# Low half of the experts' second weight brought by DMA, and the image products split over the two halves of the output partitions

## The chip, the cores and the metric

The kernel runs on one core of one Trainium2 chip. The metric is device time in microseconds of one execution, from several runs of the same program. A profile is one further execution, recorded by the hardware profiler. The engines are TensorE (PE in the profile, its weight loads PEld), VectorE (DVE), ScalarE (ACT), GpSimd (POOL) and SyncE (SP), which here only issues transfers.

## The reference, cut to what matters

Thirty-two samples of 153 tokens (25 image patches, 128 text tokens) with 192 channels are embedded, go through a quantised attention block and then through a mixture of three experts, of which one is taken for each sample:

```python
scores = softmax(mean(x, axis=1) @ Wg.T)              # x: [32, 153, 192]
sel = top_k(scores, 1)                                # one of 3 experts per sample
h = gelu(einsum('bth,ehf->betf', x, W1) + b1)         # F = 768
y = einsum('betf,efh->beth', h, W2) + b2
out = einsum('beth,be->bth', y, scores * one_hot(sel, 3))
h = h_residual + out
```

The kernel computes the expert that was taken, and no other. Float32 products are made of bf16 parts: a value is split into a high part and the remainder (the low part), and the products high x high, high x low and low x high are accumulated in PSUM.

## The kernel before, in words

The program goes through nine stages, with all engines meeting at the end of each: embedding, scales of the inputs, ranges of the hidden values, quantised q, k and v, ranges of the scores, attention, projection, the inputs of the experts (`ffn_inputs`), and `experts`. The change touches `experts` alone, which fills the last 170 us.

In `experts` every engine walks over the 32 samples (called rows here, n = 0 to 31) in an order written out by hand: `steps` writes four rows out, then a hardware loop of four rows a turn, then the last step. In step n an engine does its first job for row n and its second job for row n-1. Semaphores alone tie the engines together.

- **SyncE** (`weights`, L1824 to L1830): reads the number of the row's expert from the tile `sel` into a register (L1826, a TENSOR_LOAD in the trace), waits until row n-4's first product is done, and copies the row's first weight, high and low half, from its resident place (`vt` in the trace) into slot n mod 4 of a ring (`qk`), with two transfers of 128 x 2 x 768 bf16 (L1830). They add 16 each to the slot's semaphore `w_in`. Then `rows` (L1832) waits for row n-4's output and sends it out (L1834), and after every fourth row the image tile of the last four rows (L1838).
- **TensorE** (`first_product`, L1857): 30 matmuls of 153 columns make the 768 hidden values of the row in six chunks (L1867). `second_product` (L1871), for the row before: 18 matmuls of 192 columns (L1878) make the 128 text tokens' output in PSUM tile `p2`, from the split hidden values `gs` (`e_gs` in the trace) and the resident second weight, whose high half is `w2h` (`vbd` in the trace) and whose low half is `w2l` (`kb`). The expert is picked in both by a register in the address. Then 12 matmuls of 192 columns (L1883) make the image part: the stationary operand `gs[:, u, f, BOTH]` has 64 columns, 32 with the high part of the image tokens and 32 with their low part, and so the output lies on partitions 0 to 63 of `p3`, high part's products on 0 to 31 and low part's on 32 to 63. The last one raises `y_acc`. Before them PE waits for `i_bias`, before the 18 for `g_split` (the split hidden values) and `y_bias`.
- **ScalarE** (L1906): six GELU activations per row. Every second row starts with a table load.
- **VectorE**: `split(n)` (L1929) makes `gs` in three instructions, a cast (L1935) and two subtractions (L1937, L1938). `collect(n-1)` (L1942) reads the expert's number into a register (L1944, a TENSOR_LOAD), then adds the bias to the text output in `p2` (L1947), the bias to the image output in `p3[0:32]` (L1950), scales the text output and adds the residual (L1953), and adds `p3[32:64]` to the image tile `yi` (L1955). `yi` has 32 partitions for each of four rows, at 32*j with j = n mod 4. After j = 3, `image` (L1957) finishes the tile for four rows (L1960).

In the trace the tiles `yb`, `ot`, `yi` and `oi` all appear as `vi`, the ring of the first weight and ScalarE's output as `qk`, and all three PSUM tiles as `e_p`.

Of the kernel before, what the change touches and what calls it, by code (L numbers as in the profile page):

```python
# [7 lines left out]
ALU = mybir.AluOpType  # L8
ACT = mybir.ActivationFunctionType
F32 = mybir.dt.float32  # L10
BF16 = mybir.dt.bfloat16
# [7 lines left out]
P = 128  # L19
B, NI, NT = 32, 25, 128  # L20
# [4 lines left out]
C = 192  # L25
# [8 lines left out]
FT = FF // P  # L34
# [25 lines left out]
class Ctx:  # L60
# [8 lines left out]
    def sb(self, name, shape, dt=F32, stack=None):  # L69
        return (stack or self.stack).enter_context(self.nc.sbuf_tensor(name, shape, dt))  # L70
# [298 lines left out]
def wait_apart(eng, sem, value, passed):  # L369

    eng.wait_ge(sem, value)
    eng.sem_inc(passed, 1)
# [1410 lines left out]
def experts(k, m):  # L1783

    out, Hres = k.d["out"], m["H"]
    X, w1h, w1l, w2h, w2l, sel, gw, gwi, b2, b1s = (m[x] for x in ("X", "w1h", "w1l", "w2h", "w2l", "sel", "gw", "gwi", "b2", "b1s"))
    RING = SLOTS = 4

    HI, BOTH, LO = slice(0, NT), slice(IW, IW + 64), slice(N + 32, N + 32 + NT)
    with ExitStack() as st:  # L1790
        sb = lambda n, s, t=F32: k.sb(n, s, t, st)
        g = m["qkflat"][:, 12288:12288 + 4 * FT * N].bitcast(F32).rearrange("p (u f n) -> p u f n", u=2, f=FT)
        gs = sb("e_gs", [P, 2, FT, N + 32 + NT], BF16)
        ws = m["qkflat"][:, 0:SLOTS * 4 * FF].rearrange("p (s i a f) -> p s i a f", s=SLOTS, i=2, a=2)
        rows_out = m["vi"][:, :, :].rearrange("p a b -> p (a b)").bitcast(F32).rearrange("p (t c) -> p t c", c=C)
        share = m["line"][:, :, :].rearrange("p a b -> p (a b)")[:, 0:2 * FT * B].rearrange("p (e f b) -> p e f b", e=2, f=FT)
# [24 lines left out]
        with k.nc.Block() as block:  # L1821
            @block.sync
            def _(sp):
                def weights(n, u):  # L1824

                    e = sp.value_load(sel[0:1, ds(n, 1)], min_val=0, max_val=E - 1)  # L1826
                    if not (isinstance(n, int) and n < SLOTS):
                        wait_apart(sp, h_acc, (n - SLOTS) * 2 + 2, k.passed)
                    for i, w in enumerate((w1h, w1l)):
                        sp.dma_start(ws[:, u, i, :, :], w[:, :, e, :]).then_inc(w_in[u], 16)  # L1830

                def rows(n, j, grp):  # L1832
                    wait_apart(sp, y_out, n + 2, k.passed)
                    sp.dma_start(out[n, NI:N, :], ot[:, j, :]).then_inc(sent[j], 16)  # L1834
                    if j == 3:
                        wait_apart(sp, i_out, grp + 2, k.passed)
                        for q in range(4):
                            sp.dma_start(out[grp * 4 + q, 0:NI, :], oi[32 * q + ID:32 * q + 32, :]).then_inc(image_sent, 16)  # L1838

                def body(c, kk):  # L1840
                    now, gone = batch(c, kk, 0), batch(c, kk, 4)
                    if now is not None:
                        weights(now[0], now[1])
                    if gone is not None:
                        rows(*gone)
                steps(sp, body)
                for n in range(B - 3, B):
                    rows(n, n % 4, n // 4)
                for q in range(4):
                    sp.wait_ge(sent[q], 16 * G + 16)  # L1850
                sp.wait_ge(image_sent, 64 * G + 64)

            @block.tensor
            def _(pe):
                expert = lambda n: pe.value_load(sel[0:1, ds(n, 1)], min_val=0, max_val=E - 1)

                def first_product(n, kk):  # L1857

                    u = kk % 2
                    pe.wait_ge(h_act, n * FT + FT)  # L1860
                    pe.wait_ge(w_in[kk], (n - kk) * 8 + 32)
                    for f in range(FT):
                        o = p1[:, u, f // 3, (f % 3) * N:(f % 3 + 1) * N]
                        fs = slice(f * P, (f + 1) * P)
                        parts = ((0, 0, 0), (1, 0, 0), (0, 0, 1), (0, 1, 2), (1, 1, 2))
                        for a, (w, kt, plane) in enumerate(parts):
                            mm = pe.matmul(o, ws[:, kk, w, kt, fs], X[:, plane, ds(n * N, N)], start=(a == 0), stop=(a == len(parts) - 1))  # L1867
                        if f % 3 == 2:
                            mm.then_inc(h_acc, 1)

                def second_product(n, slot, e):  # L1871
                    pe.wait_ge(g_split, n * 2 + 2)

                    pe.wait_ge(y_bias, n + 1)
                    u = slot % 2
                    parts = [(a, w, f) for f in range(FT) for a, w in ((HI, w2h), (HI, w2l), (LO, w2h))]
                    for b, (a, w, f) in enumerate(parts):
                        mm = pe.matmul(p2[:, u, 0:C], gs[:, u, f, a], w[:, e, f, :], start=(b == 0), stop=(b == 3 * FT - 1))  # L1878

                    wait_apart(pe, i_bias, n + 1, k.passed)  # L1880
                    parts = [(w, f) for f in range(FT) for w in (w2h, w2l)]
                    for b, (w, f) in enumerate(parts):
                        mm = pe.matmul(p3[0:64, u, 0:C], gs[:, u, f, BOTH], w[:, e, f, :], start=(b == 0), stop=(b == 2 * FT - 1))  # L1883
                    mm.then_inc(y_acc, 1)

                def body(c, kk):
                    now, last = batch(c, kk, 0), batch(c, kk, 1)
                    e_last = expert(last[0]) if last is not None else None
                    if now is not None:
                        first_product(now[0], now[1])  # L1890
                    if last is not None:
                        second_product(last[0], last[1], e_last)
                steps(pe, body)
# [16 lines left out]
            def _(v):  # L1910
# [31 lines left out]
                def collect(n, j, grp):  # L1942
                    u, r = j % 2, slice(32 * j, 32 * j + 32)
                    e = v.value_load(sel[0:1, ds(n, 1)], min_val=0, max_val=E - 1)  # L1944
                    v.wait_ge(y_acc, n + 1)
                    v.wait_ge(y_out, n + 1)
                    v.tensor_tensor(yb[:, u, :], p2[:, u, 0:C], b2[:, e, :], ALU.add).then_inc(y_bias, 1)  # L1947

                    v.wait_ge(i_out, grp + 1)
                    v.tensor_tensor(yi[r, :], p3[0:32, u, 0:C], b2[0:32, e, :], ALU.add).then_inc(i_half, 1)  # L1950
                    v.wait_ge(y_bias, n + 3)
                    v.wait_ge(sent[j], (n - j) * 4 + 16)
                    v.scalar_tensor_tensor(ot[:, j, :], yb[:, u, :], gw[:, ds(n, 1)], Hres[:, n, :], ALU.mult, ALU.add).then_inc(y_out, 1)  # L1953
                    v.wait_ge(i_half, n + 1)
                    v.tensor_tensor(yi[r, :], p3[32:64, u, 0:C], yi[r, :], ALU.add).then_inc(i_bias, 1)  # L1955

                def image(grp):  # L1957
                    v.wait_ge(i_bias, grp * 4 + 6)
# [140 lines left out]
```

## Time and profile before

| | |
|---|---|
| median of 3 runs | 1036.82 us |
| lowest and highest | 1031.38 us, 1037.0 us |
| the profiled execution's own time | 1037.42 us |
| its span, first to last instruction | 1035.6 us |
| mean granted clock of TensorE | 0.837 |
| busy in the span | PE 707.6, DVE 881.2, ACT 711.9, POOL 170.0 us |
| `experts` in the span | from about 865 us to the end |

The profiled execution's time is 1.8 us more than its span, which begins and ends with an instruction, and 0.6 us above the median. Busy time is time in which an engine executes instructions of its own; reading a register, waiting and issuing transfers are not in it, and in the timeline and the chain of waits they appear with a q behind the engine's name or as "issue". Granted clock 1.0 is 2.4 GHz and 0.5 is 1.2 GHz.

### The profile page before, as it was taken

What the parts mean: (1) busy time and instruction counts of PE and PEld (TensorE: products, weight loads), DVE (VectorE), ACT (ScalarE), POOL (GpSimd) and SP (SyncE); (2) the same over time, 40 slices, a digit from 0 to 9 for tenths busy, and PEclk for the clock granted to TensorE, in tenths of its full rate; (3) what the DMA queues carried; (4) which work ended last, traced back from release to release, by engine and by line L of the source; (5) the groups of instructions that cost most, each with busy time, mean ns of one, the idle gap of its engine ahead of it and who ended that gap; (6) DMA issues with size and microseconds to landing.
All of it is one profiled execution on the core that took longest, in us unless ns stands there. A gap on an engine that the chain in (4) does not pass through costs nothing. (4 is left out here: it accounts for less than half of the span.)

```text
span 1035.6 us, 22661 instructions
## 1 busy us (share of the span) xinstructions
PE 707.6 (68%) x5955; PEld 482.3 (47%) x5956; DVE 881.2 (85%) x2422; ACT 711.9 (69%) x1376; POOL 170.0 (16%) x274
## 2 busy tenths in 40 slices
PE   3783386747888366676667666676635385999997
PEld 3562244425555233443334333343323244989996
DVE  6888997888888799999999999999978864666766
ACT  0335465957888699898988889999945294555553
POOL 5851410016664000000000000000004530000000
PEclk9985598988999687778887887877756597999999
DMA  8000000001111111111111111111022004355452
GB/s 256 3 2 0 0 1 1 0 1 39 37 37 37 36 28 24 27 25 23 25 24 24 24 24 24 24 23 24 12 89 78 18 1 152 135 186 204 165 197 83
DMA packets 84271, 54.71 MB, mean 53 GB/s; under 512 B 53704, under 2 KB 83176, under 8 KB 83976
## 3 DMA queue, kind: packets, MB, share of 16 engines
q1 hardware_dynamic: 83208, 54.11, 17.2%
q0 software_dynamic: 1024, 0.13, 0.3%
q8 instruction: 18, 0.29, 0.1%
q14 instruction: 21, 0.17, 0.1%
HBM read 11.90 MB, written 3.76 MB: 15 GB/s over the span
## 5 line engine op out<-in xcount | busy, mean ns | idle before, releaser
L1357 DVE SCALAR_TENSOR_TENSOR expo<-expo,con,pow 128x153 f32<-128x153 f32 x480 | 146.1, 374 | 0.8 <-ACT expo L1266 0.8
L1140 PE MATMUL at_rem<-word,ident_half 128*128 128x459 f16 x160 | 66.4, 415 | 102.7 <-ACT expo L1266 101.5
L1266 ACT ACTIVATE expo<-at_rem,con 128x459 f32<-128x459 f32 x160 | 95.4, 640 | 14.5 <-PE at_rem L1141 13.7
L952 DVE TENSOR_REDUCE rs_ends<-rs_banks 128x770 f32 (+1 forms) x96 | 89.2, 957 | 13.5 <-PE rs_banks L924 11.4
L873 ACT ACTIVATE rs_banks<-rs_banks 128x770 f32<-128x770 f32 x96 | 74.6, 796 | 23.2 <-PE rs_banks L916 22.1
L1222 ACT ACTIVATE word<-at_banks 128x459 uint8<-128x459 f32 x160 | 81.0, 560 | 10.4 <-PE at_banks L779 10.2
L1400 DVE CUSTOM_DVE_ANT_0 weight_top<-weight_top,line 128x2448 uint16<-128x2448 uint16 x64 | 86.1, 1345 | 2.1 <-ACT line L1258 2.1
L1140 PEld LDWEIGHTS at_rem<-word,ident_half 128*128 128x128 f16 x160 | 15.7, 98 | 152.8 <-ACT expo L1266 148.1
L1258 ACT ACTIVATE line<-weight_top 128x1224 f32<-128x1224 f32 x64 | 74.0, 1158 | 15.0 <-DVE weight_top L1385 14.7
L774 PE MATMUL at_banks<-pick,row_top 128*128 128x459 bf16 x160 | 73.1, 457 | 11.0 <-ACT word L1222 4.0
L1906 ACT ACTIVATE qk<-e_p,b1s 128x153 f32<-128x153 f32 x192 | 58.9, 392 | 29.3 <-PE e_p L1867 28.1
L1867 PE MATMUL e_p<-X,qk 128*128 (+1 forms) x960 | 72.6, 235 | 7.7 <-DMA qk<-vt 6.9
L1867 PEld LDWEIGHTS e_p<-X,qk 128*128 128x128 bf16 x960 | 66.0, 100 | 13.7 <-issue 10.4
L1215 ACT ACTIVATE pT_all<-at_pT 128x768 bf16<-128x768 int16 (+2 forms) x128 | 71.8, 637 | 0.8 <-PE at_pT L1157 0.6
L1453 POOL PARTITION_ALL_REDUCE pj_mm<-pj_mm x1 | 0.4, 356 | 418.6 <-DVE pj_mm L1527 418.6
L1385 DVE TENSOR_TENSOR weight_top<-expo,inv_total 128x1224 f32<-128x1224 f32 x64 | 68.2, 1106 | 0.0
L1141 PE MATMUL at_rem<-octave,octave_step 128*128 128x459 f16 x160 | 67.8, 424 | 0.0
L1157 PE MATMUL at_pT<-identb,weight_top 128*128 128x128 bf16 x480 | 52.0, 271 | 20.8 <-ACT pT_all L1215 19.7
L1906 ACT ACT_TABLE_LOAD x16 | 20.5, 1283 | 55.4 <-PE e_p L1867 55.4
L779 PE MATMUL at_banks<-kb,qk 128*128 128x153 bf16 x384 | 56.1, 263 | 0.0
L1878 PE MATMUL e_p<-vbd,e_gs 128*128 x384 | 53.1, 246 | 3.8 <-DVE e_gs L1938 3.8
L684 ACT ACTIVATE qi<-pq,biasp,ap 128x306 int16<-128x306 f32 x96 | 48.0, 727 | 11.1 <-PE pq L642 11.1
(390 smaller groups left out, 2085.2 us busy)
## 6 DMA issues: line engine op xcount, KB each, us to landing
qk<-vt SPq DMA_DIRECT2D x64, 384.0 KB, 3.1
rs_kb<-qk SPq DMA_DIRECT2D x128, 28.7 KB, 1.9
kb<-qk SPq DMA_DIRECT2D x128, 28.7 KB, 1.9
patches<-in_patches SPq DMA_DIRECT2D x4, 768.0 KB
vi<-vt SPq DMA_DIRECT2D x32, 96.0 KB, 2.0
out<-vi SPq DMA_DIRECT2D x32, 96.0 KB, 1.8
pj_w<-in_w SPq DMA_DIRECT2D x1, 2304.0 KB, 8.2
qb<-qk SPq DMA_DIRECT2D x128, 6.0 KB, 1.8
```

The lines of the kernel that those rows point to most:

```text
L774: pe.matmul(bank[:, 0:3 * N], top, pick[:, 3 * i:3 * i + 3, :].rearrange("p w n -> p (w n)"), start=True, stop=False, skip_group_check=True)
L873: act.activation(banks[:, s, :, 0:5 * W], banks[:, s, 1, 0:5 * W].unsqueeze(1).to_broadcast([P, 2, 5 * W]), ACT.Relu).then_inc(split, 1)
L952: v.tensor_reduce(ends[:, :, n, 5 * b:5 * b + 5], banks[:, slot(u, b), :, 0:5 * W].rearrange("p i (t n) -> p i t n", n=W), AX, ALU.max).th ...
L1140: pe.matmul(out, identh[:, :], bank(word, b).bitcast(F16), start=True, stop=False)
L1215: rank = lambda out, x: act.activation(out, x.bitcast(I16), ACT.Copy, bias=RANKS)
L1222: act.activation(dist[:, 3 * b:3 * b + 3, :], banks[:, b % 3, 0:3 * N].rearrange("p (t n) -> p t n", n=N), ACT.Copy, scale=per_step).then_ ...
L1258: act.activation(flat(line, halves[h]), flat(top, halves[h]), ACT.Copy, scale=LOWER / 3.0, bias=1.5 * LOWER).then_inc(y_done, 1)
L1266: act.activation(bank(ex, b), rem[:, (u + b) % 2, 0:3 * N], ACT.Square, scale=2.0 ** 24, bias=c(5)).then_inc(sq_done, 1)
L1357: ins = v.scalar_tensor_tensor(ex[:, t, :], ex[:, t, :], c(7), pw[:, t, :].bitcast(BF16), ALU.add, ALU.mult, accum_out=tot[:, t:t + 1])
L1400: v.tensor_tensor(flat(top, half).bitcast(I32), flat(top, half).bitcast(I32), flat(line, half).bitcast(I32), ALU.add).then_inc(i_done, 1)
L1867: mm = pe.matmul(o, ws[:, kk, w, kt, fs], X[:, plane, ds(n * N, N)], start=(a == 0), stop=(a == len(parts) - 1))
L1906: act.activation(g[:, u, f, :], p1[:, u, f // 3, (f % 3) * N:(f % 3 + 1) * N], ACT.Gelu, bias=b1s[:, f, ds(n, 1)]).then_inc(h_act, 1)
```

## The change

The image part of the second product is written as six pairs. In a pair, one matmul multiplies the 64 stationary columns with the high half of the weight and writes partitions 0 to 63 of `p3`, and the other multiplies the same 64 columns with the low half and writes partitions 64 to 127. Before, both were accumulated on partitions 0 to 63. The number of matmuls, 12, and their columns stay.

The low half of the weight for this part no longer comes from `kb` through a register in the address. It is copied per row by a third transfer (128 x 1152 bf16, contiguous on each side) to one of four places `wl`: two in a new tile `e_w2_low`, two in the tile `line`. SyncE waits for `y_acc` of row n-4 before it, and `w_in` now counts 48 per turn of the ring.

On VectorE, `collect` gets one more addition per row, of `p3[64:96]` into `yi`. It waits for the addition before it. Partitions 96 to 127 of `p3`, the product of the two low parts, are not read; before, that product was part of what L1955 added.

```diff
--- before.py
+++ after.py
@@ -1791,6 +1791,9 @@
         sb = lambda n, s, t=F32: k.sb(n, s, t, st)
         g = m["qkflat"][:, 12288:12288 + 4 * FT * N].bitcast(F32).rearrange("p (u f n) -> p u f n", u=2, f=FT)
         gs = sb("e_gs", [P, 2, FT, N + 32 + NT], BF16)
+        wl_own = sb("e_w2_low", [P, 2, FT, C], BF16)
+        wl_line = m["line"][:, :, :].rearrange("p a b -> p (a b)")[:, 2 * FT * B:2 * FT * B + FT * C].bitcast(BF16).rearrange("p (u f c) -> p u f c", u=2, f=FT)
+        wl = [wl_own[:, 0, :, :], wl_own[:, 1, :, :], wl_line[:, 0, :, :], wl_line[:, 1, :, :]]
         ws = m["qkflat"][:, 0:SLOTS * 4 * FF].rearrange("p (s i a f) -> p s i a f", s=SLOTS, i=2, a=2)
         rows_out = m["vi"][:, :, :].rearrange("p a b -> p (a b)").bitcast(F32).rearrange("p (t c) -> p t c", c=C)
         share = m["line"][:, :, :].rearrange("p a b -> p (a b)")[:, 0:2 * FT * B].rearrange("p (e f b) -> p e f b", e=2, f=FT)
@@ -1828,6 +1831,9 @@
                         wait_apart(sp, h_acc, (n - SLOTS) * 2 + 2, k.passed)
                     for i, w in enumerate((w1h, w1l)):
                         sp.dma_start(ws[:, u, i, :, :], w[:, :, e, :]).then_inc(w_in[u], 16)
+                    if not (isinstance(n, int) and n < SLOTS):
+                        wait_apart(sp, y_acc, n - SLOTS + 1, k.passed)
+                    sp.dma_start(wl[u], w2l[:, e, :, :]).then_inc(w_in[u], 16)
 
                 def rows(n, j, grp):
                     wait_apart(sp, y_out, n + 2, k.passed)
@@ -1858,7 +1864,7 @@
 
                     u = kk % 2
                     pe.wait_ge(h_act, n * FT + FT)
-                    pe.wait_ge(w_in[kk], (n - kk) * 8 + 32)
+                    pe.wait_ge(w_in[kk], (n - kk) * 12 + 48)
                     for f in range(FT):
                         o = p1[:, u, f // 3, (f % 3) * N:(f % 3 + 1) * N]
                         fs = slice(f * P, (f + 1) * P)
@@ -1878,9 +1884,9 @@
                         mm = pe.matmul(p2[:, u, 0:C], gs[:, u, f, a], w[:, e, f, :], start=(b == 0), stop=(b == 3 * FT - 1))
 
                     wait_apart(pe, i_bias, n + 1, k.passed)
-                    parts = [(w, f) for f in range(FT) for w in (w2h, w2l)]
-                    for b, (w, f) in enumerate(parts):
-                        mm = pe.matmul(p3[0:64, u, 0:C], gs[:, u, f, BOTH], w[:, e, f, :], start=(b == 0), stop=(b == 2 * FT - 1))
+                    for f in range(FT):
+                        pe.matmul(p3[0:64, u, 0:C], gs[:, u, f, BOTH], w2h[:, e, f, :], start=(f == 0), stop=(f == FT - 1))
+                        mm = pe.matmul(p3[64:128, u, 0:C], gs[:, u, f, BOTH], wl[slot][:, f, :], start=(f == 0), stop=(f == FT - 1))
                     mm.then_inc(y_acc, 1)
 
                 def body(c, kk):
@@ -1951,8 +1957,10 @@
                     v.wait_ge(y_bias, n + 3)
                     v.wait_ge(sent[j], (n - j) * 4 + 16)
                     v.scalar_tensor_tensor(ot[:, j, :], yb[:, u, :], gw[:, ds(n, 1)], Hres[:, n, :], ALU.mult, ALU.add).then_inc(y_out, 1)
-                    v.wait_ge(i_half, n + 1)
-                    v.tensor_tensor(yi[r, :], p3[32:64, u, 0:C], yi[r, :], ALU.add).then_inc(i_bias, 1)
+                    v.wait_ge(i_half, n * 2 + 1)
+                    v.tensor_tensor(yi[r, :], p3[32:64, u, 0:C], yi[r, :], ALU.add).then_inc(i_half, 1)
+                    v.wait_ge(i_half, n * 2 + 2)
+                    v.tensor_tensor(yi[r, :], p3[64:96, u, 0:C], yi[r, :], ALU.add).then_inc(i_bias, 1)
 
                 def image(grp):
                     v.wait_ge(i_bias, grp * 4 + 6)
```

Where the instructions stand, before and now, at three places (rows are an engine's instructions in program order; a line number, the operation, output<-inputs and sizes; ISA and REGISTER_ALU are register work).

TensorE, from the last text matmul into the image part, in the written-out rows; before:

```order
L1878 MATMUL e_p<-vbd,e_gs 128x192
L1883 MATMUL e_p<-vbd,e_gs 64x192 [waits e_i_bias]
L1883 MATMUL e_p<-kb,e_gs 64x192
L1883 MATMUL e_p<-vbd,e_gs 64x192
L1883 MATMUL e_p<-kb,e_gs 64x192
```

and now (five further pairs follow the first):

```order
L1884 MATMUL e_p<-vbd,e_gs 128x192
L1888 MATMUL e_p<-vbd,e_gs 64x192 [waits e_i_bias]
L1889 MATMUL e_p<-e_w_low,e_gs 64x192
L1888 MATMUL e_p<-vbd,e_gs 64x192
L1889 MATMUL e_p<-e_w_low,e_gs 64x192
```

The order of high and low stays; the second of each pair reads the copied weight and writes the other half of the partitions.

VectorE, one `collect` and the start of the next `split`; before:

```order
L1944 TENSOR_LOAD sel [waits e_g_split]
L1944 ISA x2
L1947 ISA [waits e_y_out,e_y_acc]
L1947 TENSOR_TENSOR vi<-e_p,b 128x192
L1950 TENSOR_TENSOR vi<-e_p,b 32x192 [waits e_i_out]
L1953 SCALAR_TENSOR_TENSOR vi<-vi,gw,Hres 128x192 [waits e_sent0,e_y_bias]
L1955 TENSOR_TENSOR vi<-e_p,vi 32x192 [waits e_i_half]
L1935 CAST e_gs<-qk 128x6x153 [waits e_y_acc,e_h_act]
```

and now:

```order
L1950 TENSOR_LOAD sel [waits e_g_split]
L1950 ISA x2
L1953 ISA [waits e_y_out,e_y_acc]
L1953 TENSOR_TENSOR vi<-e_p,b 128x192
L1956 TENSOR_TENSOR vi<-e_p,b 32x192 [waits e_i_out]
L1959 SCALAR_TENSOR_TENSOR vi<-vi,gw,Hres 128x192 [waits e_sent0,e_y_bias]
L1961 TENSOR_TENSOR vi<-e_p,vi 32x192 [waits e_i_half]
L1963 TENSOR_TENSOR vi<-e_p,vi 32x192 [waits e_i_half]
L1941 CAST e_gs<-qk 128x6x153 [waits e_y_acc,e_h_act]
```

One instruction, L1963, stands between the old last addition and the next row's cast.

SyncE, one turn of the loop's first row; before:

```order
L1830 ISA [waits e_h_acc]
L1830 DMA qk<-vt 128x2x768
L1830 ISA
L1830 DMA qk<-vt 128x2x768
L371 REGISTER_ALU
L1834 ISA [waits e_y_out]
L1834 DMA out<-vi 128x192
```

and now:

```order
L1833 ISA [waits e_h_acc]
L1833 DMA qk<-vt 128x2x768
L1833 ISA
L1833 DMA qk<-vt 128x2x768
L371 REGISTER_ALU
L1836 ISA [waits e_y_acc]
L1836 DMA e_w_low<-kb 128x1152
L371 REGISTER_ALU
L1840 ISA [waits e_y_out]
L1840 DMA out<-vi 128x192
```

The third transfer and its wait stand between the first weight's transfers and the sending of a finished row.

## Rows read from the trace of the kernel before

**Rows 1.** The page: busy time, and the chain that ended last by engine.
```profile
PE 707.6 (68%) x5955; PEld 482.3 (47%) x5956; DVE 881.2 (85%) x2422; ACT 711.9 (69%) x1376; POOL 170.0 (16%) x274
...
PE 10%; issue 2%; DVE 2%; ACT 1%; DVEq 1%; DMA 0%; SPq 0%; ACTq 0%
```

**Rows 2.** Busy time by windows: stretch, length, each engine's busy us, clock, DMA share, GB/s.
```profile
893.00:1031.00 138.00, 133.69 (x1665) 121.89 (x1662) 95.75 (x207) 67.40 (x179) 0.00 (x0) 1.00 0.48 169
243.00:342.00 99.00, 78.93 (x736) 54.17 (x734) 88.43 (x99) 87.15 (x129) 54.29 (x140) 1.00 0.18 36
```

**Rows 3.** Timeline of PE, one row: start us, us, engine, line, operation.
```profile
926.35 0.25 PE L1878 MATMUL e_p<-vbd,e_gs 128*128 x1
...
927.93 0.27 PE L1883 MATMUL e_p<-vbd,e_gs 128*64 x1
...
928.86 0.25 PE L1883 MATMUL e_p<-kb,e_gs 128*64 x1
929.04 2.17 PE L1867 MATMUL e_p<-X,qk 128*128 x30
931.05 0.25 PE L1878 MATMUL e_p<-vbd,e_gs 128*128 x1
```

**Rows 4.** Timeline of DVE, j = 0 and j = 1; idle before in brackets.
```profile
922.51 0.36 DVE L1947 TENSOR_TENSOR vi<-e_p,b 128x192 f32<-128x192 f32 x1 [1.06 <-issue]
...
923.57 0.35 DVE L1955 TENSOR_TENSOR vi<-e_p,vi 32x192 f32<-32x192 f32 x1
923.85 0.62 DVE L1935 CAST e_gs<-qk 128x918 bf16<-128x918 f32 x1
...
927.13 0.36 DVE L1947 TENSOR_TENSOR vi<-e_p,b 128x192 f32<-128x192 f32 x1 [1.40 <-issue]
...
927.90 0.42 DVE L1953 SCALAR_TENSOR_TENSOR vi<-vi,gw,Hres 128x192 f32<-128x192 f32 x1
928.35 0.35 DVE L1955 TENSOR_TENSOR vi<-e_p,vi 32x192 f32<-32x192 f32 x1
928.73 0.64 DVE L1935 CAST e_gs<-qk 128x918 bf16<-128x918 f32 x1
```

**Rows 5.** Timeline of DVE: casts of four rows, an early one, the last bias.
```profile
884.55 0.64 DVE L1935 CAST e_gs<-qk 128x918 bf16<-128x918 f32 x1 [2.49 <-ACT qk L1906]
...
919.56 0.64 DVE L1935 CAST e_gs<-qk 128x918 bf16<-128x918 f32 x1
...
933.59 0.64 DVE L1935 CAST e_gs<-qk 128x918 bf16<-128x918 f32 x1 [0.34 <-ACT qk L1906]
...
938.74 0.63 DVE L1935 CAST e_gs<-qk 128x918 bf16<-128x918 f32 x1
...
1030.52 0.36 DVE L1947 TENSOR_TENSOR vi<-e_p,b 128x192 f32<-128x192 f32 x1 [0.46 <-PE e_p L1883]
```

**Rows 6.** Waits of DVE, 893 to 1032 us: who <- whom, us in total, times, longest.
```profile
DVE vi L1947 <- issue: 32.8, 28, 1.5
DVE e_gs L1935 <- ACT qk L1906: 3.1, 7, 0.7
```

**Rows 7.** The line that reads the expert's number on DVE: ns min/median/max.
```profile
L1944 DVEq TENSOR_LOAD <-sel x32: 300/311/778, 879.6 to 1029.4; - x32
```

**Rows 8.** Start of the stage in the chain; a smaller transfer from the page.
```profile
865.82 0.75 SPq L1830
...
866.71 3.11 DMA qk<-vt
...
vi<-vt SPq DMA_DIRECT2D x32, 96.0 KB, 2.0
```

**Rows 9.** Timeline of PE in the attention, 64 stationary columns.
```profile
499.86 0.32 PE L1173 MATMUL at_out<-pT_all,v_image_row 128*64 128x128 bf16 x2
499.97 0.23 PE L1174 MATMUL at_out<-pT_all,v_image_row 128*64 128x25 bf16 x2
```

**Rows 10.** Windows, columns as in rows 2: the clock there.
```profile
499.40:502.60 3.20, 3.07 (x28) 1.83 (x27) 3.20 (x18) 2.66 (x6) 0.00 (x0) 0.50 0.07 24
```

## Prediction

> **What bounds the kernel now.** The page comes first: VectorE is busy for most of the span, yet the chain that ended last runs over TensorE, and shares of a whole program say little about its last stage [rows 1]. So the windows view is read for this stage: in 138 us TensorE is busy 133.7, VectorE 95.8 and ScalarE 67.4, with the clock at its upper level throughout [rows 2]. By busy time alone TensorE is the limit and VectorE has 42 us to spare. The timelines of the two engines say otherwise.
>
> TensorE's row [rows 3]: from the first text matmul at 926.35 to the first image matmul at 927.93 is 1.58 us, from there to the next row's first product at 929.04 is 1.11, and from there to the next text matmul at 931.05 is 2.01. A row takes 4.70 us, four rows 18.8. The twelve image matmuls start 0.085 us apart ((928.86 - 927.93)/11 = 0.93/11), and 0.18 us pass from the last of them to the first product.
>
> VectorE's row: cast to cast is 923.85 - 919.56 = 4.29 us in the step that collects a row with j = 0, then 928.73 - 923.85 = 4.88, then 4.86 with a wait of 0.34 for ScalarE in it, then 5.15, which has the image instruction [rows 4, 5]. Four rows take 938.74 - 919.56 = 19.18 us, and of these VectorE waited for another engine for 0.34. What looks like idle time is not slack: the 1.06 or 1.40 us before each L1947 [rows 4] is called "issue", it sums to 32.8 us over 28 rows [rows 6], and it is the sequence that reads the expert's number, with a register load of 0.30 to 0.78 us in it [rows 7]. It stands in every row, also in those in which nothing was late. So VectorE's own sequence needs 19.18 - 0.34 = 18.84 us for four rows, and TensorE's 18.8: **two engines are at the limit together**. Over the whole stretch VectorE waited for ScalarE 3.1 us in 7 places [rows 6]; that is all it has left.
>
> **TensorE's part of the change.** Twelve matmuls become six pairs on separate halves of the output partitions. The attention has such pairs: two matmuls with 64 stationary columns form one piece of 0.32 us, and the next two begin 0.11 us later (499.86 to 499.97) [rows 9]. The clock was at its lower level, 1.2 GHz [rows 10], where 128 columns need 0.107 us, so the pair took the time of one matmul. I take the same here: six pairs at 0.085 us, 5 intervals instead of 11, and the image part goes from 1.11 to about 0.60 us. It saves 0.51 us a row; TensorE's row becomes 4.20 us, four rows 16.8. The bounds are 0 (the pairs run one behind the other) and 0.51.
>
> **VectorE's part.** One addition of 32 x 192 is added per row. Its nearest row is L1955, 0.35 us, with the same shapes and the same tiles [rows 4]. What it adds to the row is the distance from one start to the next. The rows show two cases: at 923.57 the next instruction starts after 0.28 us, at 928.35 after 0.38 [rows 4], so the bounds are 0.28 and 0.38. I take 0.38, because the new instruction waits for the one ahead of it, and its input is on other partitions than that one's, as where L1955 follows L1953 (0.42 long, start to start 0.45).
>
> The Trainium skill has a rule for just this ("VectorE: DVE Perf Modes", section "Two Vector instructions with no wait between them"): an instruction starts only after all earlier ones have finished if its input or output starts in another group of 32 partitions than the last one's from the same memory, and may otherwise start earlier. The rows agree: short distances only where the tile's quarter is the first, long ones elsewhere. By the rule the new addition is held in every row (its input starts at partition 64, the last one's at 32), and 32 rows cost 12.2 us; if it weren't held, 9.0.
>
> Now the cover. 32 additions by 0.38 are 12.2 us on VectorE. Off it come the waits that they fill: 3.1 us for ScalarE [rows 6]; the first row's addition, which lies in the wait of 2.49 us before 884.55 [rows 5], 0.4; the start of the third first product, which follows the first, shortened image part, 0.5, and brings that wait's end forward; and the wait for TensorE before the last L1947, 0.46 [rows 5], of which 0.4 is filled while TensorE comes earlier. That is 4.4, and **7.8 us are left**. TensorE's 0.51 us a row buys nothing else: with 16.8 us against VectorE's 18.84 + 4 x 0.38 = 20.4 for four rows, it will wait about 0.9 us in each row for the split values.
>
> **SyncE and the transfers.** The third transfer is 288 KB, between 96 KB, which lands in 2.0 us, and 384 KB, which lands in 3.1 [rows 8]. In the first row it delays the start, since TensorE waits for three transfers: the chain goes over the second one's landing, and one issue takes 0.75 us and 0.89 from start to start (865.82 to 866.71) [rows 8]. So the start comes about **0.8 us later**; bounds 0 and 1.5 (issue and data behind each other). Later rows hide it. It waits for row n-4's second product, two rows, some 10 us, before row n's first product; behind it SyncE has only the sending of row n-4, which waits for VectorE's later work on the same row anyway. One more issue of 0.75 us beside two fits into a row of 5 us. Cover gone, a late weight would cost its lateness once per row.
>
> The transfer has a second effect. The idle before L1947 is 1.06 in one row and 1.40 in the next [rows 4]; (32.8 - 28 x 1.06)/0.34 gives some 9 long ones of 28. The long ones come while weights are in flight. The DMA share rises from 0.48 [rows 2] by 288/768 of nearly all of it, to about 0.6. I count no change in the number of long loads, since the third transfer is issued at another place of the row; the bounds are 9 fewer (-3 us) and 20 more (+7 us).
>
> **The sum** is 7.8 + 0.8 = 8.6 us against the profiled execution's 1037.42, so 1046.0. That execution is 0.6 us above the median, and for the median I forecast 1036.8 + 8.6 = **1045.4 us**. What a measurement of this kernel can tell from no change is about 1%, 10.4 us: the forecast lies inside, not far from its edge (1047.2).
>
> **Rivals.** (1) *VectorE has slack after all*, chance 0.07. The idle stretches would shrink under pressure, and TensorE's gain would appear: some 28 rows by 0.51 less 0.8, so 1023 us. For it speaks the chain, which names mostly TensorE [rows 1]; against it that 1.06 us recurs where all inputs were there, and the 19.18 against 18.84 above. It decides if VectorE can do four rows with the additions in under 18.8 us.
>
> (2) *The register load becomes long in most rows*, chance 0.17. The third transfer would be in flight when VectorE reads the number; 20 more long loads at 0.34 are 6.8 us, so 1052. It passes the edge of 1% from about 5 more long loads on. Against it: the median load is short today, 311 ns [rows 7], though transfers take half the time. The Trainium skill ("DMA: Bandwidth & Descriptors", section "Latency and other measured facts") gives such a load a floor of about 600 ns; by that all would be long already, and the trace, with 300 ns, disagrees.
>
> (3) *The pairs don't overlap*, the change doing nothing for TensorE, chance 0.05. TensorE's 18.8 us for four rows is still under VectorE's 20.4; only the two gains at the start and the end go, +0.9, so 1046.3.
>
> (4) *A weight arrives late or TensorE's clock falls*, chance 0.06 in all. TensorE idle for 0.9 us of 5.1 would be busy 0.82 of the time. In the ranges stage it was busy 0.80 of 99 us with the clock at its upper level [rows 2]. One fall over a row would cost that row some 4 us; a weight late by 1 us in each row would end at 1070.
>
> The forecast itself has 0.63, between 1041 and 1049; 0.02 is left for a gain that I don't see. From these: faster by over 1% 0.08 (rival 1 and part of the rest), within 1% 0.55 (four fifths of the forecast, most of rival 3), slower by over 1% 0.37. The range for 8 in 10 leaves out rival 1 and the worst of 4 and takes in rival 2 and the low bounds (9 short loads, a start that isn't later): 1038 to 1053 us.
>
> **What the profile after would show.** Right: L1963 in 32 instances of about 0.35 us with about 0.03 us before it; cast to cast of four rows 20.0 to 20.8 us; no wait of VectorE for ScalarE past the first rows; the image part of TensorE 0.6 us long, and before each first text matmul a wait of nearly 1 us for VectorE's L1944; the chain mostly on VectorE and issue; the first product starting 0.8 us later. Wrong: idle before VectorE's bias addition under 1 us (rival 1) or 1.4 in most rows (rival 2), image matmuls 0.085 us apart (rival 3), first products waiting for a transfer after the first row (rival 4).

## The result, and the profile after the change

| | before | after |
|---|---|---|
| median of the runs | 1036.70 us (4 runs) | 1049.61 us (4 runs, 1048.05 to 1050.5) |
| ratio, 95% interval | | 1.0122 [1.0106, 1.0138] |
| span of the profiled execution | 1035.6 us | 1046.2 us |
| first register load of SyncE to the end | 170.75 us | 184.79 us |

The change costs **12.9 us** in the medians, 1.2%, inside the range and with the sign of the forecast, 4.3 us more than the 8.6 of its sum: the additions on VectorE are the cost, as forecast, and the cover that was taken off them did not come. This is just over the bound of 1%. The stage itself is 14.0 us longer. The profiled execution began it 3.4 us earlier (861.46 against 864.87 us), which has nothing to do with the change; so parts of the stage are compared below, not whole spans.

The page after, busy time and chain; they answer to [rows 1]:

```profile
PE 695.0 (66%) x5955; PEld 464.6 (44%) x5956; DVE 892.1 (85%) x2454; ACT 710.9 (68%) x1376; POOL 167.2 (16%) x274
...
issue 6%; DVE 6%; DVEq 3%; PE 1%; DMA 0%; ACT 0%; SPq 0%; ACTq 0%
```

TensorE, 10% of the chain before, has 1%. VectorE, its queue and "issue" have the rest. The windows view after, columns as in [rows 2]: the middle of the stage and its last product.

```profile
893.00:1041.00 148.00, 125.03 (x1649) 107.01 (x1647) 104.39 (x232) 66.30 (x175) 0.00 (x0) 0.99 0.57 206
```
```profile
1036.70:1040.00 3.30, 3.22 (x22) 2.80 (x24) 1.83 (x5) 0.00 (x0) 0.00 (x0) 0.50 0.06 19
```

The DMA share rose from 0.48 to 0.57. In the last product the granted clock was 0.50, the lower level, after TensorE had waited up to 2.6 us for VectorE. The waits after, 893 to 1041 us, which answer to [rows 6]:

```profile
DVE vi L1953 <- issue: 34.6, 28, 1.6
...
PE e_p L1873 <- issue: 11.2, 24, 0.7
PE e_p L1884 <- DVE e_gs L1944: 9.9, 20, 2.6
```

VectorE's waits for ScalarE have gone from this stretch. TensorE waits 9.9 us for VectorE's split values, and 11.2 us for nothing but its own queue, in front of the first product. The second of these waits was not foreseen. VectorE's timeline over two rows (start, duration, line), which answers to [rows 4, 5]:

```profile
940.83 0.63 DVE L1941 CAST e_gs<-qk 128x918 bf16<-128x918 f32 x1
...
951.01 0.64 DVE L1941 CAST e_gs<-qk 128x918 bf16<-128x918 f32 x1
951.68 0.96 DVE L1943 TENSOR_TENSOR e_gs<-qk,e_gs 128x768 bf16<-128x768 f32 x1
952.56 0.35 DVE L1944 TENSOR_TENSOR e_gs<-qk,e_gs 128x192 bf16<-128x192 f32 x1
954.12 0.36 DVE L1953 TENSOR_TENSOR vi<-e_p,b 128x192 f32<-128x192 f32 x1 [1.21 <-issue]
954.51 0.35 DVE L1956 TENSOR_TENSOR vi<-e_p,b 32x192 f32<-32x192 f32 x1
954.90 0.42 DVE L1959 SCALAR_TENSOR_TENSOR vi<-vi,gw,Hres 128x192 f32<-128x192 f32 x1
955.34 0.35 DVE L1961 TENSOR_TENSOR vi<-e_p,vi 32x192 f32<-32x192 f32 x1
955.73 0.35 DVE L1963 TENSOR_TENSOR vi<-e_p,vi 32x192 f32<-32x192 f32 x1
956.33 0.64 DVE L1941 CAST e_gs<-qk 128x918 bf16<-128x918 f32 x1 [0.24 <-issue]
...
961.87 0.63 DVE L1941 CAST e_gs<-qk 128x918 bf16<-128x918 f32 x1
```

Four rows take 961.87 - 940.83 = 21.04 us (before 19.18, forecast 20.4, and 20.0 to 20.8 among the signs of being right). The new addition L1963 starts 0.39 us after L1961, as forecast. One thing is new: the cast at 956.33 comes 0.60 us after L1963 instead of 0.38, with 0.24 of "issue", and the loop's branch stands there. The 1.56 us between the starts of L1944 and L1953 are not new in kind: the same stretch took 1.29 to 1.88 us before, and its sum over 31 rows rose from 46.9 to 50.0 us. TensorE's timeline at an image part, which answers to [rows 3]:

```profile
944.48 0.27 PE L1888 MATMUL e_p<-vbd,e_gs 128*64 x1
944.48 0.27 PE L1889 MATMUL e_p<-e_w_low,e_gs 128*64 128x192 bf16 x1
944.59 0.25 PE L1888 MATMUL e_p<-vbd,e_gs 128*64 x1
944.59 0.25 PE L1889 MATMUL e_p<-e_w_low,e_gs 128*64 128x192 bf16 x1
...
944.92 0.25 PE L1889 MATMUL e_p<-e_w_low,e_gs 128*64 128x192 bf16 x1
945.47 1.23 PE L1873 MATMUL e_p<-X,qk 128*128 x15 [0.31 <-issue]
```

The two halves start at the same time, pairs are 0.08 to 0.11 us apart, six pairs start within 0.44 us. And yet 0.99 us pass from the image part's start to the next first product, at best from the third row on (0.62 us stands once, in the second row); the median from 893 us on is 1.20 us, where it was 1.11. The start of the stage in the chain, and VectorE's register load, which answer to [rows 8] and [rows 7]:

```profile
863.27 0.64 SPq L1833
864.04 3.08 DMA e_w_low<-kb
867.12 0.14 issue
867.26 2.10 PE e_p L1873 x15
```
```profile
L1950 DVEq TENSOR_LOAD <-sel x32: 301/358/1048, 877.3 to 1039.5; - x32
```

From SyncE's first register load to the first product it is 867.26 - 861.46 = 5.80 us, before 5.08. The register load's mean rose from 422 to 486 ns, the worst from 778 to 1048.

### The profile page after: what moved, and what is told of

It reads as the page before. It is cut to its first block and busy times, and to the rows that moved or that the text cites. A ratio compares the mean times of both kernels' runs of the same rounds, so it can differ in the third digit from the quotient of the medians.

```text
span 1046.2 us, 22827 instructions
## 1 busy us (share of the span) xinstructions
PE 695.0 (66%) x5955; PEld 464.6 (44%) x5956; DVE 892.1 (85%) x2454; ACT 710.9 (68%) x1376; POOL 167.2 (16%) x274
## 5 line engine op out<-in xcount | busy, mean ns | idle before, releaser
L1873 PE MATMUL e_p<-X,qk 128*128 (+1 forms) x960 | 73.6, 236 | 22.0 <-issue 12.9
L1157 PE MATMUL at_pT<-identb,weight_top 128*128 128x128 bf16 x480 | 52.2, 271 | 20.8 <-ACT pT_all L1215 19.8
L1884 PE MATMUL e_p<-vbd,e_gs 128*128 x384 | 55.3, 250 | 11.0 <-DVE e_gs L1944 10.9
```

## The experiments

Twelve kernels, in three groups. Each group shared its runs of the kernel before (1036.76, 1037.36 and 1036.20 us). "Theory V", "theory A" and so on are names that each expectation explains. Two numbers are read from each trace beside the time: the **24 rows** from the sixth to the thirtieth cast, as the mean of four rows (before 19.53 us, after 21.07), and the distance from the start of an image part to the next first product (median from 893 us on, before 1.11, after 1.20).

**The change taken apart: additions and transfer.** First the two halves put into the kernel before, each alone.

```
a3, before with a second addition        a4, before with the third transfer
+ tensor_tensor(yi, p3[32:64], yi)       + dma_start(wl[u], w2l[:, e]) in SyncE's weights()
                                           (wl is brought and not read)
```

> The kernel before with one more addition per row on VectorE: p3[32:64] is added to the image tile a second time, each waiting for the one ahead (so the image part of the output counts that piece twice). Theory V (VectorE's own sequence sets the row): four rows take 18.5 us with short register loads plus 4 x 0.385, so 20.1 to 20.7 us, and the run is 8 to 10 us slower than before, nearly all of what the change costs; TensorE's image part stays at 1.11 us. Theory T (the third transfer is the cost, by long register loads and a late start): this run has no such transfer and is within 3 us of before.

Measured: 1049.55 us, ratio 1.0122 [1.0108, 1.0136], four rows 20.94 us. The additions alone give 12.8 us (1049.55 - 1036.76), as much as the whole change, and more than the 8 to 10 us of theory V; the four rows, too, lie above its 20.1 to 20.7.

> The kernel before with the third transfer per row and its wait for y_acc, and w_in counted with it; nobody reads what it brings. Theory V: the start is 0.7 us later and the register loads on VectorE cost up to 0.1 us a row more, so 1 to 4 us slower. Theory T: 8 to 13 us slower.

Measured: 1040.37 us, 1.003 [1.0008, 1.0052], four rows 20.13 us: 3.6 us, within theory V's 1 to 4, though not for its reasons, as shown below. Then the change without the one or the other (a1 leaves out the product rows of partitions 64 to 95, a2 takes the low half of expert 0 in every row):

```
a1  - tensor_tensor(yi[r, :], p3[64:96, u, 0:C], yi[r, :], ALU.add)
a2  - dma_start(wl[u], w2l[:, e, :, :])
    - matmul(p3[64:128, u], gs, wl[slot][:, f, :])
    + matmul(p3[64:128, u], gs, w2l[:, 0, f, :])
```

> The changed kernel without its new addition (the product of the high hidden part with the weight's low half is made but left out of the image output). Theory V: VectorE's row is as before, 18.5 to 19.2 us for four rows, and no wait for ScalarE is left in it; the time is within 4 us of before on either side, though TensorE's image part is 0.5 us a row shorter. Theory P (TensorE set the row before): 10 us or more faster than before. Theory T: 8 us or more slower than before.

Measured: 1041.61 us, 1.0043 [1.0029, 1.0058], four rows 20.14 us: the pairs were there and the new addition was not, and it was still 4.8 us slower than before. That is outside theory V's 4 us, and so are the four rows (18.5 to 19.2). That TensorE's saving would appear as soon as VectorE is spared the addition is refuted.

> The changed kernel without the third transfer: the paired matmuls read the low half of expert 0's weight at a fixed address for every row (so that piece of the image output is of the wrong expert where another was taken). Theory V: 1 to 4 us faster than the changed kernel, by the start (0.7 us) and shorter register loads on VectorE; four rows 20.4 to 20.8 us. Theory T: within 2 us of the kernel before.

Measured: 1048.51 us, 1.0107 [1.0089, 1.0124], four rows 20.94 us. In the change the transfer costs about 1 us, most of it the later start (0.72 us).

Additions and transfer don't add up: 12.8 and 3.6 alone, 12.9 together. And a1 and a4 have the same four rows, 20.1 us, with and without pairs. Neither VectorE's additions nor the length of the image part sets them. The chain of a4 from 920 to 1000 us, by line, and SyncE's queue over one row (start, duration):

```profile
by line: SPq L1833 23.1%; issue 17.3%; SPq L1829 16.3%; SPq L1836 9.9%; SPq L1840 9.2%; SPq L1844 6.4%; PE e_p L1884 5.8%; PE e_p L1873 5.4%; PE e_p L1889 4.2%; SPq L371 1.3%; SPq L372 1.0%; SPq L1812 0.5%
...
949.73 0.88 SPq L1829
...
951.16 0.68 SPq L1833
...
951.99 0.64 SPq L1833
...
952.83 0.52 SPq L1836
...
953.63 0.49 SPq L1840
...
954.25 0.89 SPq L1829
```

A row of **SyncE's queue** takes 954.25 - 949.73 = 4.5 us without a wait in it: the register load of the expert's number 0.88, two weights, the low half (953.63 - 952.83 = 0.80 from its start to the next), the output. With the four image outputs of each fourth row (L1844), 2.3 us, four rows make some 20 us. SyncE's waits for VectorE's results show its slack, before and in a4, 893 to 1020 us (in a1 they are 0.7 us, in the change 6.4 us):

```profile
SPq L372 <- DVE vi L1953: 18.8, 14, 2.5
```
```profile
SPq L372 <- DVE vi L1966: 0.4, 1, 0.4
```

So there is a third queue at 20.0 us for four rows. The change hid it behind VectorE's 21.07.

**The order of the additions.** Does the place of the new addition matter?

```
b1  p3[32:64] is added before the text's scaling, p3[64:96] after it
```

> The changed kernel with VectorE's five instructions of collect in another order: p3[0:32], text bias, p3[32:64], text scaling, p3[64:96], so that none waits for the one just ahead of it. Theory V says that the additions cost their length and that the chained wait costs 0.22 us more once per four rows, where the loop's branch, executed before in the shadow of an instruction, comes only after the wait: four rows 0.2 us shorter (21.05 to about 20.8), the run 1 to 3 us faster than the changed kernel. If the chained waits were a large part of the price, each row would lose more than 0.1 us and the run would be 4 us or more faster.

Measured: 1050.02 us, 1.0132 [1.0094, 1.0169], four rows 20.90 us. Four rows are 0.17 us shorter, about the 0.2 expected: where the loop's branch stands, the next cast follows the last addition after 0.39 us, in the change after 0.61. The 1 to 3 us in the time did not show.

**VectorE's register load moved.** The idle "issue" before the bias addition is the register load and what its use needs. In c1 (from the kernel before) and c2 (from the change) it is put behind the issue of the big subtraction, so that it runs beside those 0.96 us; c3 is c2 with b1's order.

```
  v.tensor_tensor(gs[..., LO], g, gs[..., HI], ALU.subtract)     (0.96 us)
+ e = v.value_load(sel[0:1, ds(last, 1)])
  v.tensor_tensor(gs[..., N:N+32], ...)                          (0.35 us)
  ...
- e = v.value_load(sel[0:1, ds(n, 1)])
  v.tensor_tensor(yb[:, u, :], p2[:, u], b2[:, e, :], ALU.add)
```

> The kernel before with one thing moved: VectorE reads the expert's number for collect while the large subtraction of split runs, instead of after split has ended. Theory V: VectorE's four rows fall from 18.5 to 19.2 us to about 16 (0.7 us a row less, and long loads mostly covered), TensorE's 18.8 are then the bound, and the run is 4 to 7 us faster than before, not more. Theory P (VectorE was never at the limit): within 1 us of before.

Measured: 1039.11 us, 1.0027 [1.0012, 1.0043], four rows 19.87 us. The 4 to 7 us that the expectation has for freeing VectorE alone did not come; it is 1.7 us slower. Its chain and its new wait:

```profile
by line: PE e_p L1867 43.6%; PE e_p L1878 31.0%; PE e_p L1883 22.1%; issue 3.3%
```
```profile
DVE e_gs L1935 <- ACT qk L1906: 22.7, 14, 2.4
```

VectorE has gained 22.7 us of waiting for ScalarE, and nearly all of the chain is TensorE: in the kernel before, two engines were at the limit, as the prediction said. What made it slower is in TensorE's own queue, 893 to 1020 us, once in each turn of the loop; before it was 0.5 us in 2 places:

```profile
PE e_p L1867 <- issue: 3.8, 6, 0.8
```

> The changed kernel with the same early reading of the expert's number. Theory V: VectorE's four rows fall from 21.05 to about 17.6 us, and now the shorter image part counts: TensorE's four rows of 16.8 are under that. The run is about 24 us faster than the changed kernel and 7 to 14 us faster than before, so faster than the kernel before with the early load. If the long register loads were the cost and not the sequence, only half a row's 0.2 us would come back: 6 us faster than the changed kernel. If something else binds at 4.7 us a row (weights, ScalarE), it ends equal to c1.

Measured: 1041.16 us, 1.0038 [1.002, 1.0055], four rows 20.01 us. It is 8 us faster than the change, where the expectation has 24: with SyncE's 20.0 us in the way, that is all that the 21.07 can give back. The bound is SyncE's queue again, and the low half comes late:

```profile
by line: SPq L1833 27.7%; issue 20.5%; SPq L1829 19.8%; SPq L1836 10.7%; SPq L1840 10.3%; SPq L1844 7.7%; SPq L371 1.6%; SPq L372 1.1%; SPq L1812 0.7%
```
```profile
PE e_p L1873 <- DMA e_w_low<-kb: 7.1, 8, 1.6
```

> c2 and the order of b1 together. Theory V: another 0.2 us for four rows, 1 to 2 us faster than c2; equal to c2 if TensorE or ScalarE binds there by then.

Measured: 1039.68 us, 1.0031 [1.0014, 1.0048], four rows 20.01 us: as c2; the intervals overlap.

**TensorE's register load moved.** TensorE reads the same number before each first product. Moved behind the first product's issue:

```
- e_last = expert(last[0])      (ahead of first_product)
  first_product(...)
+ e = expert(n)                 (at the head of second_product)
  pe.wait_ge(g_split, ...)
```

> The change with one instruction sequence moved: TensorE's sequencer reads the expert's number (its register load, 0.30 to 0.31 us, up to 1.09) before the wait of the second product, and no longer before the first product of the next row. Theory A (VectorE sets the row after the change, and the pairs' 0.51 us stops first at TensorE's sequencer): from the start of an image part to the next first product falls from a median of 1.20 us to 0.6 to 0.8, VectorE's queue stays as it was at 21.0 us per four rows, and the time is that of the change, 1049.6 us, give or take 1.5. Theory B (the pairs' gain is withheld only by that register load): the 24 rows in the middle fall from 126.4 us towards 117, and the time to 1037 to 1042. Theory C: the load then stands in front of the second product and lengthens the row by up to 0.3 us where the image part of the row before ends late: 1050 to 1058.

Measured: 1050.29 us, 1.0125 [1.0107, 1.0144], four rows 21.12 us, image part to first product 0.62 us. Theory A to the number: the 0.5 us appears at once when the register load is gone from that place, and goes into TensorE's wait for VectorE's split, 893 to 1020 us (6.3 us in the change over the same stretch):

```profile
PE e_p L1885 <- DVE e_gs L1944: 19.6, 23, 1.6
```

> The kernel before, with VectorE's register load behind the big subtraction (as in c1, 1039.1 us, where TensorE was the chain all through at 4.70 to 4.97 us per row and one of 5.3 to 5.9 at each loop branch) and TensorE's register load moved behind the first product. Theory A (TensorE's own sequencer was what kept c1 from gaining): image start to next first product stays near 1.11 us, since sequential matmuls fill it, the long gaps at the loop branch (0.57 to 0.95 us) go, four rows fall from 19.9 to 19.0 to 19.5 us, and the time is 1032 to 1037 us. Theory B (the load lands in front of the second product and costs there what it saved): 1038 to 1041 us. Theory C (VectorE is still the bound): as before, 1037 us.

Measured: 1034.94 us, 0.9984 [0.9969, 0.9999], four rows 19.35 us, image part to first product 1.11. Inside theory A's numbers: 1.3 us faster than before. The only thing that c1 lacks is TensorE's moved register load, and with it the 3.8 us of c1's queue are gone. Now TensorE's products fill nearly the whole chain from 920 to 1000 us. A row of them still takes the prediction's 4.7 us; what makes 19.35 of its 18.8 is the first text matmul, which comes 0.2 to 0.4 us late in 8 of 27 rows:

```profile
by line: PE e_p L1867 43.1%; PE e_p L1879 32.5%; PE e_p L1884 23.6%; issue 1.0%
```

> The change, with VectorE's and TensorE's register loads moved as in e2. In c2 (VectorE's load alone) the chain was SyncE's queue, some 20 us per four rows with three weight transfers a row, and the time 1041.2 us. Theory A (SyncE's queue is then the bound): the 24 rows in the middle stay at 119 to 121 us, TensorE waits for the third transfer in several rows, and the time is 1040 to 1043 us. Theory B (TensorE's sequencer was the bound in c2): with the pairs now felt, 24 rows of 112 to 117 us, 1033 to 1038 us.

Measured: 1039.5 us, 1.0035 [1.0018, 1.0052], four rows 20.01 us, 23.1% of the chain in SyncE's L1833. Theory A's bound, half a microsecond under its range of times; the waits for the third transfer rose to 9.6 us in 9 places.

**SyncE relieved as well.** e6 is e5 with the third transfer issued by GpSimd, idle in this stage; everything of the change is computed. Two other things move with it: TensorE waits for the low half before the second product and no longer before the first, and the cast's semaphore is folded into `g_split`.

```
- sp.dma_start(wl[u], w2l[:, e, :, :]).then_inc(w_in[u], 16)
+ @block.gpsimd:  e = po.value_load(sel[...]); wait for y_acc and for the transfer ahead
+                 po.dma_start(wl[u], w2l[:, e, :, :]).then_inc(w_low, 16)
+ second_product:  pe.wait_ge(w_low, n * 16 + 16)
```

> As e5, with the third transfer of a row issued by GpSimd, which does nothing else in this stage, one at a time, so that SyncE's queue is that of the kernel before; TensorE waits for it behind the first product. Theory A (pairs pay only when VectorE's load, TensorE's load and SyncE's queue are all out of the way): VectorE's own work is then the bound, four rows 19.0 to 19.9 us, 24 rows 114 to 119.5 us, and the time 1034 to 1040 us, at or under e2's only if TensorE was e2's bound by more than VectorE's two additions (0.77 us a row). Theory B (VectorE's additions make it longer than TensorE's shortened part whatever the queues do): four rows 20.0 to 20.5 us and 1040 to 1044 us, above e2. Theory C (GpSimd's issue is slow, and TensorE waits for the low half): waits of over 0.5 us a row for that transfer, 1045 to 1060 us.

Measured: **1030.47 us, 0.9945 [0.9928, 0.9962]**, four rows 18.59 us, image part to first product 0.62. It beats the kernel before by 5.7 us and the change by 19; e2, which has everything but the change itself, is 4.5 us slower, and their intervals don't meet. Theory A's condition held, since the pairs pay once the three queues are out of the way, but its bound did not: the time is 3.5 us under its range, and four rows are 18.6 us instead of 19.0 to 19.9. VectorE's own work, which theory A took for the bound, needs about 17.6 us by an estimate, since VectorE still waits 6.8 us for ScalarE in 7 places from 893 to 1020 us, and the chain from 920 to 1000 us goes back and forth between TensorE (58%), VectorE and ScalarE, so that no engine's own row is the bound:

```profile
by line: PE e_p L1885 26.8%; PE e_p L1898 22.9%; issue 12.7%; PE e_p L1902 8.2%; ACT qk L1925 6.8%; DVE e_gs L1954 5.6%; DVEq L1957 5.6%; DVE e_gs L1958 3.2%; DVE vi L1969 1.6%; DVE vi L1977 1.4%; DVE vi L1979 1.0%; DVE e_gs L1956 0.5%; ACT
```

VectorE's row in e6 with j = 0, the shortest of the four, columns as before:

```profile
954.26 0.64 DVE L1954 CAST e_gs<-qk 128x918 bf16<-128x918 f32 x1
954.93 0.96 DVE L1956 TENSOR_TENSOR e_gs<-qk,e_gs 128x768 bf16<-128x768 f32 x1
955.81 0.35 DVE L1958 TENSOR_TENSOR e_gs<-qk,e_gs 128x192 bf16<-128x192 f32 x1
956.50 0.36 DVE L1969 TENSOR_TENSOR vi<-e_p,b 128x192 f32<-128x192 f32 x1 [0.34 <-DVE e_gs L1958]
...
957.57 0.35 DVE L1977 TENSOR_TENSOR vi<-e_p,vi 32x192 f32<-32x192 f32 x1
957.95 0.35 DVE L1979 TENSOR_TENSOR vi<-e_p,vi 32x192 f32<-32x192 f32 x1
958.23 0.64 DVE L1954 CAST e_gs<-qk 128x918 bf16<-128x918 f32 x1
```

From the small subtraction to the bias addition it is 0.69 us instead of 1.4 to 1.9, and this row with both additions takes 3.97 us (4.80 in the change, 945.63 - 940.83). GpSimd's issues of 0.55 us stand beside everything else, and SyncE has part of its slack back (893 to 1020 us):

```profile
POOL e_w_low L1868 <- PE e_p L1903: 39.9, 10, 4.3
```
```profile
SPq L372 <- DVE vi L1975: 9.8, 9, 3.7
```

## Why the prediction was right, and where it was off

- **VectorE's additions: right.** 0.38 us each by forecast, 0.39 by the trace, 12.2 us for 32. a3 alone gives 12.8. That VectorE and TensorE are at the limit together is shown by a3, where more work on VectorE costs its full length, and by c1: with VectorE freed, TensorE takes the chain and nothing is gained. The rows of 18.8 us are the undisturbed ones, and the stretch chosen was a short one: it took 19.18 us, the mean over 24 rows is 19.53, and with both register loads moved it is still 19.35 (e2).
- **The cover of 4.4 us: the step that was off.** The ScalarE waits did go, 3.1 us, but more came back: the stage after its start is 13.3 us longer, where 7.8 stood. Added up over the starts of VectorE's instructions, the new addition has 12.4 us, the stretch from the small subtraction to the bias addition 3.1 more, the last wait for TensorE 0.6, the second cast 0.4, against 2.9 less before the other casts and 0.3 in the rest: 13.3. So nothing was covered on balance. The trace has these pieces: the loop's branch, which such a wait had hidden, 0.22 to 0.29 us in 6 places, 1.4; the longer register loads, 32 x (486 - 422) ns, 2.0; the text part of the last second product at the lower clock, 2.98 us instead of the other rows' 1.61, 1.4; the stretch from L1944 to L1953 in rows with j = 0, where 0.1 us more stands in 8 rows without a longer load, 0.8, for a reason that stays open. Together 5.6 against the 5.5 missing. Of these the branch is tested (b1), the others are read; a3 shows that most of them come with the additions and not with the transfer, since its 24 rows are 8.4 us longer than before's and the change's 9.2.
- **The pairs: the 0.51 us are right as a duration, wrong as the place where they stop.** I had them stop at the wait for VectorE. They stop a step earlier, at TensorE's register load before the first product, a queue that I never priced (e1, where it is moved away: 0.62 us). For the time it made no difference, VectorE being later than both. The change with a faster VectorE (c2) shows no gain over the kernel before either, but there SyncE's queue is the bound, so what TensorE's register load alone would cost it is not shown.
- **The start: right.** 0.72 us, forecast 0.8.
- **"One more issue fits into a row of 5 us": wrong, and hidden.** By itself the third transfer on SyncE makes four rows 20.0 us (a1, a4, c2, e5), 0.5 to 0.6 us over the kernel before's 19.53. It cost nothing because the additions took 21.07, and that was luck. I had counted the two other issues and left out SyncE's own register load of 0.88 us, the distances between issues, and the four image outputs.
- **Rivals.** (1) is refuted by a3 and e1: one more addition in each row costs its full length, so there was no slack where "issue" stood, and freeing TensorE changes nothing. (2) happened in small: the loads got longer, 2.0 us. (3) is refuted by the timeline. (4) happened in small, one weight late by 0.9 us and one part at the lower clock. The likeliest case said within 1%; the result lies at 1.2%, on the side that had 0.37.

## What to carry to other kernels

Before a change moves work between engines, write down for each engine *and each queue* what one round takes, register loads, branches and DMA issues included: here VectorE, TensorE, its sequencer and SyncE lay so close (18.8 to 20.0 us for four rows, before the additions come on top) that relieving one alone gained nothing against the kernel before (a1, c1, c2, e1), relieving two left +3.3 us (e5), and relieving three at once turned +12.9 us into -5.7. An idle time that the profile calls "issue" is neither slack nor fixed: look for what the sequencer does there, and put it beside a long instruction that is already issued. When a saving appears in no run, follow it from its place to the first thing that starts later than it could.

## What the runs showed of the hardware

- **The register load of the expert's number is not a constant.** On VectorE it took 0.30 to 1.05 us in the change, on SyncE 0.27 to 0.91 with a median of 0.87 in a4 (0.56 in the kernel before), on GpSimd 0.28 to 0.92 in e6. In SyncE's queue the long ones follow soon after its own weight transfers, the short ones come behind the image outputs (0.88 against 0.46 us in a4). That the transfers lengthen it is not tested by itself. The Trainium skill's "DMA: Bandwidth & Descriptors" (section "Latency and other measured facts") has a floor of about 600 ns; half of VectorE's are at 0.36 or below.
- **The issuing engine matters although the transfers share the DMA engines.** By the Trainium skill ("DMA: Bandwidth & Descriptors", section "Issuing engines are not separate DMA queues") issuing from several engines saves only the sequencer's time for it, "which is usually small relative to the DMA itself". The trace agrees on what is saved and not on its weight: the transfer takes 3.0 us and is mostly hidden, while the queue's time for it, 0.8 us a row, made SyncE the bound, and moving it gave 9.0 us (e5 to e6). Those 9.0 us include the later wait of TensorE for the low half. The runs don't separate the two, but e5's four rows are SyncE's own 20.01 us with 1.7 us of slack in 127, which a later wait alone would not shorten.
- **A wait on the instruction just ahead holds back what follows in the queue**, the loop's branch too: in the change the branch begins 0.09 us behind the start of the last addition, and the next cast comes 0.22 us later than in other rows. In b1, where the last addition doesn't wait for the one just ahead, it doesn't come later.
- **The clock fell once after the stage's start**, which runs at 0.50 in both kernels: after TensorE had waited 2.6 us for VectorE in the last rows, the next part ran at a granted clock of 0.50, 1.2 GHz, and took 2.98 us.
